# A graph-attention and message-passing kernel: softmax sums kept in the chain, skip layer moved, turned one-hots built from loaded numbers

## What is computed

```python
q = (x @ Wq.T + bq).reshape(N, H, C)            # N 3125, H 4, C 32
k = (x @ Wk.T + bk).reshape(N, H, C)
v = (x @ Wv.T + bv).reshape(N, H, C)
alpha = jnp.sum(q[dst] * k[src], axis=-1) / np.sqrt(C)
m = jax.ops.segment_max(alpha, dst, num_segments=N)
e = jnp.exp(alpha - m[dst])
z = jax.ops.segment_sum(e, dst, num_segments=N)
a = e / z[dst]
out = jax.ops.segment_sum(a[:, :, None] * v[src], dst, num_segments=N)
conv = out.reshape(N, H * C) + x @ Wskip.T + bskip
out1 = conv @ Wout.T + bout
out2 = layer_norm(out1 + x)
out4 = layer_norm(relu(out2 @ W1.T + b1) @ W2.T + b2 + out2)
x = layernorm(x + out4)
```

## Time and profile before

| | |
|---|---|
| median of 3 runs | 2289.12 us (2287.69 to 2289.96) |
| the profiled execution's own time | 2279.33 us |
| its span | 2277.5 us |
| busy: PE, DVE, ACT, POOL | 1772.7, 1680.3, 1215.9, 1566.1 us |
| instructions: PE, DVE, ACT, POOL | 11969, 4672, 3032, 1618 |
| mean granted clock of TensorE | 0.963 of full speed |
| DMA | 242.98 MB, mean 107 GB/s |

### The profile page before, as it was taken

One profiled execution on the slowest core, in us unless ns is written; L12 is line 12 of the kernel. 1 busy time (PEld: TensorE's weight loads), 2 busy tenths in 40 slices (PEclk: granted clock), 3 DMA queues, 4 the chain that ended last, 5 costly groups with the idle time before them and its releaser, 6 DMA issues. The chain is left out here.

```text
span 2277.5 us, 42009 instructions
## 1 busy us (share of the span) xinstructions
PE 1772.7 (78%) x11969; PEld 1412.4 (62%) x11969; DVE 1680.3 (74%) x4672; ACT 1215.9 (53%) x3032; POOL 1566.1 (69%) x1618
## 2 busy tenths in 40 slices
PE   5576677777776777777798888888888888888885
PEld 4466666666666666666675565565566565565564
DVE  4777777777777777888665777777777777777776
ACT  3566666566566566664255454444544544545443
POOL 4777777777777777775003777777777777777772
PEclk8799999999999999999898999999999999999998
DMA  8656555565555555654001222222222222222221
GB/s 264 169 160 174 160 164 167 157 174 158 168 161 162 168 160 162 170 161 143 1 16 42 56 57 57 57 56 57 56 56 58 56 57 56 57 56 56 56 56 44
DMA packets 213737, 242.98 MB, mean 107 GB/s; under 512 B 42992, under 2 KB 173254, under 8 KB 213124
## 3 DMA queue, kind: packets, MB, share of 16 engines
q0 software_dynamic: 64480, 158.57, 25.8%
q1 hardware_dynamic: 149028, 81.73, 12.4%
HBM read 228.18 MB, written 11.94 MB: 105 GB/s over the span
## 5 line engine op out<-in xcount | busy, mean ns | idle before, releaser
L437 POOL DMA_INDIRECT rows<-kv_tab,src_col x806 | 787.4, 977 | 271.8 <-issue 259.9
L452 POOL DMA_INDIRECT rows<-up_tab,src_col x806 | 765.6, 950 | 273.0 <-issue 245.5
L503 PE MATMUL ps<-hots,msg 128*128 128x128 f32 x1616 | 344.2, 296 | 288.7 <-DVE msg L1034 277.2
L701 PE MATMUL ps<-hotT,hots 128*128 128x128 f32 x3232 | 425.5, 286 | 127.9 <-DVE hots L1318 127.6
L701 PEld LDWEIGHTS ps<-hotT,hots 128*128 128x128 f32 x3232 | 388.6, 196 | 203.9 <-DVE hots L1318 203.3
L503 PEld LDWEIGHTS ps<-hots,msg 128*128 128x128 f32 x1616 | 254.3, 198 | 328.0 <-DVE msg L1034 320.7
L1049 DVE TENSOR_TENSOR acc<-acc,ps 128x256 f32 x808 | 333.9, 413 | 29.8 <-PE ps L503 5.9
L1282 DVE TENSOR_TENSOR acc<-acc,ps 128x256 f32 x808 | 332.4, 411 | 3.5 <-PE ps L701 1.8
L751 ACT COPY hotT<-ps 128x512 f32<-128x512 f32 x202 | 118.4, 586 | 404.4 <-PE ps L485 398.9
L503 PE MATMUL ps<-hots,exb 128*128 128x128 f32 x1616 | 324.1, 283 | 0.0
L1297 DVE TENSOR_TENSOR hots<-rows,yvec 128x384 f32<-128x384 f32 x202 | 114.6, 567 | 241.8 <-DMA rows<-up_tab,src_col 241.7
(11 more groups left out here) (163 smaller groups left out, 2467.4 us busy)
## 6 DMA issues: line engine op xcount, KB each, us to landing
qwin<-q_tab SPq DMA_DIRECT2D x808, 64.0 KB
rows<-kv_tab,src_col POOLq DMA_INDIRECT x806
rows<-up_tab,src_col POOLq DMA_INDIRECT x806
hots<-emb_rows SPq DMA_DIRECT2D x202, 16.0 KB
weights<-r_far SPq DMA_DIRECT2D x25, 128.0 KB, 3.4
emb_rows<-weights SPq DMA_DIRECT2D x25, 128.0 KB
kv_tab<-rows SPq DMA_DIRECT2D x12, 256.0 KB, 2.8
dst_lanes<-in_dst_lanes SPq DMA_DIRECT2D x30, 65.0 KB
```

The lines of the kernel that those rows point to most:

```text
L437: nc.gpsimd.indirect_dma_start(kvr[:, q % RING, k, :], None, kv_tab, bass.IndirectOffsetOnAxis(src_col[:, t:t + 1].bitcast(U32), 0)).then_ ...
L452: nc.gpsimd.indirect_dma_start(upr[:, q % RING, k, :], None, up_tab, bass.IndirectOffsetOnAxis(src_col[:, t:t + 1].bitcast(U32), 0)).then_ ...
L503: mm = pe.matmul(ps[:, 4 + 2 * (j % 2) + k // 2, (2 * (k % 2) + m) * P:(2 * (k % 2) + m + 1) * P], left[:, j % 2, k, :], hot_of[:, j % HOT ...
L701: mm = pe.matmul(ps[:, 4 + 2 * (q % 2) + k // 2, (2 * (k % 2) + m) * P:(2 * (k % 2) + m + 1) * P], left[:, q % 2, k, :], hot2[:, q % 2, k, ...
```

## The change

The chain has seven steps, two in a slot (`steps_at`). After the exponential, steps 3 to 5 scan for running sums as steps 0 to 2 do for maxima, carry the sum to the next batch, and divide, so that step 6 turns finished probabilities back. They stay in PSUM, and `weigh` reads them there with a broadcast, so `spread` goes. PE's `sums` has four products per quad, `acc` keeps only the message sums in pass one, and `add_tile` adds 128 x 128. The turned one-hots are no longer turned by PE: SP broadcasts each quad's relative destinations (bfloat16, 128 KB, `rel`) from a new DRAM row `rel_far`, which DVE computes and SP stores at the start, and ACT makes a square and a relu of 128 x 512. In `product`'s slot the order on DVE is weigh, first add, product, chain, two adds, scores, last add, second chain step. Batches are of 8 quads up to 192, then 5 and 5 (26 in all); RING is 20; two quads are weighed in slots 198 and 200 and from 202 on. x by Wskip plus its bias is computed in seven slots between 20 and 32 of pass one, over `xT`. In the dense stage denominators, inverses and `divide` go; `attended` adds `acc` and the skip rows, `first_out` has one product per tile, and POOL adds bout to a second copy of x. POOL thus makes two additions of 128 x 3200 behind its last gather of pass one. In the last loop each chunk has its own moments and scales: `final_sum` waits for no normalising, and ACT takes the next chunk's root ahead of normalising this one.

```diff
-STARTS = [*range(0, 161, BQ), *range(166, 199, 4)]
+STARTS = [*range(0, 193, BQ), 197]
 STOPS = STARTS[1:] + [NQ]
 BATCHES = len(STARTS)
-RING = 16
-HOTS = 17
+RING = 20
+HOTS = 4
...
-DOUBLES = (178, 184, 190, 196)
+DOUBLES = (198, 200)
...
-        for _ in range(2 if slot in DOUBLES or slot >= NQ + CHAIN else 1):
+        for _ in range(2 if slot in DOUBLES or slot >= NQ else 1):
...
-            sp.wait_ge(q_out, 16 * len(fours))
+            sp.wait_ge(rel_ready, 2)
+            sp.dma_start(rel_far.rearrange("(p n) -> p n", p=RP), rel_rows).then_inc(q_out, 16)
+            sp.wait_ge(q_out, 16 * (len(fours) + 1))
+            sp.dma_start(wskip, a["weights"][:, W_SKIP:W_SKIP + D]).then_inc(ld["w"], 16)
+            sp.dma_start(vecs[:], a["vecs"]).then_inc(ld["w"], 16)
 
             def windows(q):
                 if q >= 4:
                     sp.wait_ge(qe_ready, q - 3)
+                sp.dma_start(rel[:, q % RELS, :], rel_far[q * QC:(q + 1) * QC].partition_broadcast(P)).then_inc(q_in[q % 4], 16)
...
-                    sp.dma_start(vecs[:], a["vecs"]).then_inc(ld["const"], 16)
                     sp.dma_start(weights[:], a["weights"]).then_inc(ld["weights"], 16)
             batch_rows(BATCHES - 1)
+            sp.wait_ge(msg_ready, 186)
+            sp.dma_start(xc.rearrange("p t f -> p (t f)"), a["x_rows"]).then_inc(ld_x[0], 16)
+            sp.wait_ge(qe_ready, 200)
+            sp.dma_start(qwin[:, 3].rearrange("p t f -> p (t f)"), a["row_vecs"].partition_broadcast(P)).then_inc(ld["dense"], 16)
             sp.wait_ge(msg_ready, 190)
-            sp.dma_start(xb.rearrange("p t f -> p (t f)"), a["x_rows"]).then_inc(ld["dense"], 16)
-            sp.wait_ge(qe_ready, 200)
-            sp.dma_start(qwin[:, 3, 0:3].rearrange("p t f -> p (t f)"), a["row_vecs"].partition_broadcast(P)).then_inc(ld["dense"], 16)
...
                 for k in real_tiles(q):
@@ -438,7 +473,10 @@
                         kvr[:, q % RING, k, :], None, kv_tab,
                         bass.IndirectOffsetOnAxis(src_col[:, t:t + 1].bitcast(U32), 0)).then_inc(rows_in[q % RING], 16)
 
-            pool.wait_ge(ld["dense"], 32)
+            pool.wait_ge(ld["dense"], 16)
+            pool.wait_ge(ld_x[0], 32)
+            nc.gpsimd.tensor_tensor(xc, xc, row_bout.unsqueeze(1).to_broadcast([P, TABLE_TILES, D]), ALU.add).then_inc(xb_ready, 1)
+            pool.wait_ge(ld_x[1], 32)
...
             def sums(j):
                 pe.wait_ge(msg_ready, j + 1)
-                if j >= 2:
-                    pe.wait_ge(acc_step, adds_before(j - 1))
+                pe.wait_ge(hot_ready, j + 1)
+                if j >= SUMS:
+                    pe.wait_ge(acc_step, adds_before(j - SUMS + 1))
                 for k in range(QT):
-                    for m, left in enumerate((msg0, exb)):
-                        mm = pe.matmul(ps[:, 4 + 2 * (j % 2) + k // 2, (2 * (k % 2) + m) * P:(2 * (k % 2) + m + 1) * P],
-                                       left[:, j % 2, k, :], hot_of[:, j % HOTS, k, :], start=True, stop=True)
-                    mm.then_inc(sum_ready, 1)
-
...
+            def skip(i):
+                pe.wait_ge(ld["w"], 64)
+                if i:
+                    pe.wait_ge(skip_sb, i)
+                cols = slice(fours[i][0] * P, (fours[i][-1] + 1) * P)
+                pe.matmul(ps[:, 7, 0:len(fours[i]) * P], wskip, xT[:, cols], start=True, stop=True).then_inc(skip_mm, 1)
+
...
+                b, steps = steps_at(q)
+                if q + 1 < NQ:
                     queries(q + 1)
-                if step == 3:
-                    pe.wait_ge(ex_ready, b + 1)
-                    pe.transpose(ps[:, 3, 0:P], scr[:], ident).then_inc(probs_mm, 1)
-                if q in (NQ + 1, NQ + 3):
-                    prepare((q - NQ) // 2)
-
-
...
             def first_out(j):
                 pe.wait_ge(conv, j + 1)
@@ -583,8 +600,7 @@
                     pe.wait_ge(u1_sb, j)
                 for k, t in enumerate(chunk_tiles(j)):
                     to = ps[:, 2, k * P:(k + 1) * P]
-                    pe.matmul(to, xT[:, tile_cols(t)], wx, start=True, stop=False)
-                    mm = pe.matmul(to, convs[:, j % 2, k * P:(k + 1) * P], wt(W_OUT), start=False, stop=True)
+                    mm = pe.matmul(to, convs[:, j % 2, k * P:(k + 1) * P], wt(W_OUT), start=True, stop=True)
                 mm.then_inc(out1_mm, 1)
...
+                act.wait_ge(q_in[q % 4], 16 * (QT + 1) * (q // 4 + 1))
+                if q >= TURNS:
+                    act.wait_ge(qe_ready, q - TURNS + 1)
+                to = hotT[:, q % TURNS].rearrange("p t e -> p (t e)")
+                nc.scalar.activation(to, rel[:, q % RELS, :], ACT.Square, bias=consts[:, K_NEGP:K_NEGP + 1]).then_inc(squareT_ready, 1)
+                act.wait_ge(squareT_ready, q + 1)
+                nc.scalar.activation(to, to, ACT.Relu, bias=1.0, scale=-1.0).then_inc(hotT_ready, 1)
...
-                v.tensor_tensor(msg0[:, j % 2], kvr[:, j % RING, :, D:2 * D], exb[:, j % 2], ALU.mult).then_inc(msg_ready, 1)
+                b = batch_of(j)
+                lane = QT * (j - STARTS[b])
+                dve.wait_ge(probs_mm, b + 1)
+                if j >= 3:
+                    dve.wait_ge(sum_ready, j - 2)
+                p_of = ps[:, chain_bank(b), 0:P].rearrange("p (h t) -> p t h", h=H)[:, lane:lane + QT, :]
+                v.tensor_tensor(msg0[:, j % 3].rearrange("p t (h c) -> p t h c", h=H),
+                                kvr[:, j % RING, :, D:2 * D].rearrange("p t (h c) -> p t h c", h=H),
...
+                to = acc[:, 1, bass.ds(base[0], 1)]
+                v.tensor_scalar(to, to, sum_states[:, b % 2, 2:3], None, ALU.mult).then_inc(acc_step, 1)
...
+                if k == 0:
+                    dve.wait_ge(sum_ready, j + 1)
                 dve.wait_ge(acc_step, adds_before(j + 1) - QT + k)
-                to = acc[:, :, bass.ds(base[k], P)]
-                v.tensor_tensor(to, to, ps[:, 4 + 2 * (j % 2) + k // 2, (k % 2) * 256:(k % 2) * 256 + 256]
-                                .rearrange("p (m f) -> p m f", m=2), ALU.add).then_inc(acc_step, 1)
-
-            turned_scores, running = ps[:, 3, 0:P], ps[:, 3, 2 * P:3 * P]
...
+                if step == 3:
+                    dve.wait_ge(less_ready, b + 1)
+                    if b:
+                        dve.wait_ge(carry_sb, 2 * b)
+                        v.tensor_tensor(first_sums, carry[0:1, :], less[0:1, :], ALU.mult).then_inc(carried_ready, 1)
+                    dve.wait_ge(ex_ready, b + 1)
+                    v.tensor_tensor_scan(fw[:], same[:, 0:P], scr[:, 0:P], 0.0, ALU.mult, ALU.add).then_inc(local_ready, 1)
+                    v.tensor_tensor_scan(bw[:, ::-1], after, scr[:, 0:P][:, ::-1], 0.0, ALU.mult, ALU.add).then_inc(local_ready, 1)
+                if step == 4:
+                    dve.wait_ge(ends_sb, 2 * b + 2)
+                    if b:
+                        dve.wait_ge(carried_ready, b)
+                    v.tensor_tensor_scan(sum_fw[0:1, :], row_same[0:1, 0, :], tile_sum[0:1, 0, :], 0.0, ALU.mult, ALU.add).then_inc(row_ready, 1)
+                    v.tensor_tensor_scan(sum_bw[0:1, 0:H * HS][:, ::-1], row_same[0:1, 1, ::-1], tile_sum[0:1, 1, ::-1], 0.0,
+                                         ALU.mult, ALU.add).then_inc(row_ready, 1)
+                    dve.wait_ge(row_ready, 4 * b + 4)
+                    v.tensor_tensor(ratio[0:1, 0, :], sum_bw[0:1, 0:H * HS].rearrange("p (h t) -> p h t", h=H)[:, :, 1],
+                                    first_sums, ALU.add).then_inc(ratio_ready, 1)
+                    dve.wait_ge(ratio_ready, 3 * b + 1)
+                    v.reciprocal(ratio[0:1, 0, :], ratio[0:1, 0, :]).then_inc(ratio_ready, 1)
+                    dve.wait_ge(ratio_ready, 3 * b + 2)
+                    v.tensor_tensor(ratio[0:1, 1, :], ratio[0:1, 0, :], first_sums, ALU.mult).then_inc(ratio_ready, 1)
+                if step == 5:
+                    dve.wait_ge(back_sb, 2 * b + 2)
+                    v.tensor_tensor_scan(fw[:], same[:, 0:P], scr[:, 0:P], sum_states[:, b % 2, 0:1], ALU.mult, ALU.add).then_inc(total_ready, 1)
+                    v.tensor_tensor_scan(bw[:, ::-1], scr[:, P:0:-1], after, sum_states[:, b % 2, 1:2], ALU.add, ALU.mult).then_inc(total_ready, 1)
+                    dve.wait_ge(total_ready, 6 * b + 4)
+                    v.tensor_tensor(fw[:], fw[:], bw[:], ALU.add).then_inc(total_ready, 1)
+                    dve.wait_ge(total_ready, 6 * b + 5)
+                    v.reciprocal(bw[:], fw[:]).then_inc(total_ready, 1)
+                    dve.wait_ge(total_ready, 6 * b + 6)
+                    v.tensor_tensor(scr[:, 0:P], scr[:, 0:P], bw[:], ALU.mult).then_inc(shift_ready, 1)
 
             def pad_lanes(b):
...
+            def attended(j):
                 if j >= 2:
                     dve.wait_ge(out1_mm, j - 1)
```

(56 more changed lines are left out.)

436 lines of the change are left out of this document (197 added, 239 removed).

## The result

The changed kernel takes 2270.2 us (median of 4 runs, 2266.5 to 2273.0), the kernel before 2289.5: a ratio of 0.9924, with a 95% interval of 0.9908 to 0.9940. That is 19.3 us won where 40 were forecast. The sign was right and half of the gain is missing: the time lies outside the forecast's own 2236 to 2262, and inside the outer range of 2222 to 2273.

A forecast was written before the change was run, and what follows sets the result against it. POOL's gathers, one behind the other, were taken to bound both passes. The sum 0 - 11 - 3.5 - 16.5 - 9 = -40 took 2289.1 to 2249 us (2236 to 2262; outer range 2222 to 2273).

The forecast's parts named there:

- The start: Before quad 4's gathers: the new rel_far store lands between 37 and 43 us, POOL's wait at about 46.8; cost 0.
- Last gather to last add: End of pass one: DVE lag 11.5, work and waits 32, standstill beside POOL's additions 7; 50.5 against 54.0, -3.5 us.
- The pace: Pass one's gathers: without the weighing's two SBUF inputs, half of 21.8 us of stretch is won, -11 us.
- The rival in which the pace stays: Pass one: sum scans or something else stretch as many gathers; pace term 0, time 2260; chance 0.13.
- DVE, ACT and PE in pass one: Pass one: DVE's 3.8 of 5.0 us a slot, ACT's equal work and PE's halved products stay hidden; each 0.
- The rival in which DVE becomes the bound: Pass one: chain waits at half clock and slow weighing make a slot 5.4 us; +30, time 2319; chance 0.07.
- The dense stage: Between the passes: chunk period 13.4 to 11.5 us wins 9.5, an earlier first sum of chunk 1 wins 7; -16.5 us.
- The end: Last loop: with the waits gone, the chunk period falls from 4.06 us to DVE's 2.3; -9 us.
- The drain turns bad: Behind pass one: POOL's additions block the chain twice, +8 in place of -3.5; time 2268; chance 0.09.

The follow-up runs named there:

- both edits: Changed kernel with its three 101-partition transfers made as 96 and 5, and POOL's two additions put behind the last batch's probabilities: 2242.5 us, ratio 0.9811 to the kernel before.
- the second profile before: Another profile of the unchanged kernel before, taken on another chip: span 2284.7 us.

## Where the forecast failed, and where it held

**The start, "0, hidden": the step that failed most, +16.** "Cover: 4 us. If it is gone, each us late is a us of the time" was true, and the landing "between 37 and 43" was not: the store landed at about 62. I priced it by a store of another shape and by its bytes, and put the pass over the new rows at 33 us; it came at 48.0. The new arrays lie over 101 partitions. The load of 404 KB and the small one behind it were in 24 us behind the first issue, the store of 202 KB 11 us behind its own, and with 96 + 5 partitions the wait was gone. The Trainium skill has the rule, in "DMA: Bandwidth & Descriptors", Why a DMA increments its semaphore by 16 and not by 1: the number of engines that serve a transfer is the largest up to 16 that divides its slowest dimension on both sides. 101 is prime, so by that rule one engine serves it; the trace doesn't show the engines of one transfer, and the two landings and the split agree with it. The diff had the number in it, and I read only the size.

**Last gather to last add, "11.5 + 32 + 7 = 50.5": +10.0 in place of -3.5.** All three terms were too small. The stall was 11.0 (5.54 + 5.49), not 7; it fell on the scan and on the comparison, as "where its masks, row scans or sum scans come up against one" has it, and it is wholly undone by a later place. The lag to the last scores is 13.5 without a stall, not 11.5. The rest is 38.6, not 32: DVE's work in it was counted rightly (28.3 forecast, 27.7 found), but its waits for PE and ACT are 10.9 and not 4; one of them, between the ends' turns and the row scans, is 3.04 us alone. How much of them is the lower clock's (0.66 there, 0.90 in the same stretch before) stays open, since the products that raised it to 0.94 stood in the way of the turns. With both edits the drain is 52.1, near the 50.5, though by another sum.

**The pace, -11: right, and too careful.** -15.2. Reading SBUF again cost 20.6 us, more than the change had won, since its scans stay. In before's trace, of the 750 gathers between 100 and 1060 us, 106 started inside a DVE operation with two operands in SBUF, and 68 of them took over 1.02 us; of the 452 that started inside another one and the 192 that started inside none, not one did. The rival in which the pace stays is out. It drew on the Trainium skill's "SBUF — State Buffer", Who interferes with whom; that page's inference, that making descriptors isn't delayed by a `tensor_tensor`, does not carry over to these gathers (985 against 959 ns). The rule on GpSimd's reads in the same section of the Trainium skill holds here: 14.31 against 1.87 us. A gather also reads its row numbers from SBUF (`src_col`), so this second rule may be what stretches it; no run tells the two apart.

**DVE, ACT and PE in pass one, "0, hidden": right.** POOL's waits for weighings are 4.9 us in all, none over 0.3. The clock fell as feared, and costs at most 4 us there. The rival in which DVE becomes the bound is out on chips like the first; on the two with stops POOL does wait for weighings.

**The dense stage, -16.5: -12.9.** Both parts were mis-sized. The first sum of chunk 1 stands 4.1 behind the last add (3.5 forecast, 10.5 before). The period is 12.3, not 11.5. I had taken PE at 10.6 and DVE as next. PE is busy 11.1 a chunk (10.5 with the turn moved) and waits 1.2, of which 0.9 are a hop from its turn to ACT's copy and back. Before, the products of the inverses (L577) stood between the turn and the first hidden product; after, nothing does (PE before, then PE after):

```profile
1150.86 0.60 PE L595 MATMUL ps<-consts,hots 128*128 128x128 f32 x4
1151.29 1.06 PE L577 MATMUL ps<-consts,work 128*128 128x128 f32 x8
```

```profile
1152.18 0.60 PE L611 MATMUL ps<-consts,rows 128*128 128x128 f32 x4
1153.65 1.98 PE L619 MATMUL ps<-rows,weights 128*128 128x512 f32 x4 [0.87 <-ACT rows L855]
```

With the turn moved the period is the 11.5 of the forecast. What came late next was this hop by way of ACT; DVE comes behind it.

**The end, -9: -6.9 by the table, but the term was right.** DVE's part runs at 2.2 us a chunk (2.3 forecast). From chunk 1's `final_sum` to the end of the span it is 29.1 us in both profiles of the kernel before and 19.8 in that of the changed one, so the loop gave 9.3. The rest lies ahead of it: from pass two's last gather to that `final_sum` the profiled execution before took 12.7 us, the second profile before 15.0, the one after 15.0. In the first TensorE kept its full clock there and in the two others it did not (windows from all three, in this order):

```profile
2240.00:2248.40 8.40, 5.04 (x43) 4.66 (x42) 5.16 (x16) 0.29 (x1) 0.00 (x0) 1.00 0.00 1
2245.00:2255.60 10.60, 7.53 (x41) 7.04 (x41) 4.97 (x15) 0.29 (x1) 0.00 (x0) 0.68 0.00 1
2240.00:2250.30 10.30, 7.22 (x39) 6.87 (x39) 4.71 (x14) 0.29 (x1) 0.00 (x0) 0.67 0.00 0
```

So these 2.3 us are a difference between executions, seen between two of the kernel before alone, and not the change's.

**The rivals.** "The drain turns bad" had the right mechanism, at the right place (+8 forecast, +10 found, +8.0 against the second profile before), and its total of 2268 is near the measured one, but through another cause as well: it had no cost at the start.

## What to carry to other kernels

A new transfer is priced by its shape before its size: look at the partition count first, and give a small store that another engine waits for its own landing time from a row of the same shape. When an operation moves from SBUF to PSUM on one side, ask also what stands beside it on POOL: here the same edit decided both the pace of the gathers and 11 us of the drain. And when products go from an engine, look for the round trip that they covered; it is the next bound sooner than the engine with the next highest share.

## What the runs showed that I had not expected

- The chips differ for this program by a third. On two of them DVE stands some 11 us at a time, often with PE and ACT (in one trace 45 waits of DVE ahead of L1060 are 410 us), and the change wins nothing there. POOL's sequencer has no such stop: its idle time put down to "issue" in pass one is 244 to 254 us in all those traces, 266 on the first chip. The kernel before is slower there by as much, but there is no trace of it from those chips. What stops the engines wasn't found; the trace calls the releaser "remote" or "issue".
- A POOL addition over 128x3200 holds a DVE operation with two operands in SBUF to its very end, even one over 1x132, and leaves adds with one operand in PSUM alone.
- With TensorE at 0.71 of its clock or at 0.94, pass one takes the same time within 4 us, where POOL sets the pace. On the way into the last loop, where DVE waits for PE, 0.68 in place of 1.00 cost 2.3 us.
